# Unread TensorE products with 128 columns of weights in place of 32, in four places of a two-layer decoder kernel

## The reference

```python
logits = jnp.einsum('bsd,de->bse', x, Wg)          # routing, layer 0
top_vals, top_idx = jax.lax.top_k(logits, TOP_K)
...
att = jax.nn.softmax(jnp.einsum('blhd,bmhd->blmh', q, k) * scale, axis=2)   # cross attention
```

## Time and profile before

| what | us |
|---|---|
| median of three runs | 1131.32 |
| the three runs | 1131.32, 1134.64, 1130.4 |
| span of the profiled execution, first to last instruction (the profile gives no other time of it) | 1131.2 |
| TensorE busy in it (8612 products) | 1010.0 |
| weight loads, beside it | 719.1 |
| VectorE, ScalarE, GpSimd busy | 618.1, 425.0, 255.4 |
| mean granted clock of TensorE | 0.967 |

### The profile page before, as it was taken

One profiled execution on the slowest core, in us unless ns is written; L12 is line 12 of the kernel. 1 busy time (PEld: TensorE's weight loads), 2 busy tenths in 40 slices (PEclk: granted clock), 3 DMA queues, 4 the chain that ended last, 5 costly groups with the idle time before them and its releaser, 6 DMA issues.

```text
span 1131.2 us, 20802 instructions
## 1 busy us (share of the span) xinstructions
PE 1010.0 (89%) x8612; PEld 719.1 (64%) x8612; DVE 618.1 (55%) x1398; ACT 425.0 (38%) x557; POOL 255.4 (23%) x282
## 2 busy tenths in 40 slices
PE   6889889999987899999998798879888987986997
PEld 3666566576575799997445465747565665654566
DVE  2653753662667564333334846675575668765443
ACT  1533533524433355555541254142416231541112
POOL 0310310120130233333322020231013110210662
PEclk9999999899897899999999899999999999997999
DMA  6013413211400691111113000200020010004447
GB/s 188 1 43 126 135 43 107 89 43 44 152 1 1 254 378 57 47 48 47 43 39 98 1 2 6 85 2 5 1 76 2 6 38 1 1 2 131 130 135 236
DMA packets 64237, 80.50 MB, mean 71 GB/s; under 512 B 12736, under 2 KB 57680, under 8 KB 63120
## 3 DMA queue, kind: packets, MB, share of 16 engines
q1 hardware_dynamic: 53392, 61.15, 16.3%
q0 software_dynamic: 5664, 15.47, 4.2%
q10 hardware_dynamic: 5088, 2.56, 0.9%
HBM read 46.13 MB, written 33.03 MB: 70 GB/s over the span
## 4 chain that ended last, share of the span: by engine, by line
PE 61%; DVE 17%; ACT 12%; issue 5%; DMA 2%; POOL 2%; SPq 0%; ACTq 0%; DVEq 0%; POOLq 0%
PE ps L1522 8%; PE ps L1857 7%; DVE sb_arena L874 6%; ACT sb_arena L645 6%; PE ps L1658 5%; PE ps L1680 4%; PE ps L1885 4%; PE ps L1868 3%; PE ps L1728 3%; PE ps L1783 3%; DVE sb_arena L878 3%; PE ps L1566 2%; PE ps L1995 2%; PE ps L1630 2%; PE ps L1905 2%
## 5 line engine op out<-in xcount | busy, mean ns | idle before, releaser
L645 ACT ACTIVATE sb_arena<-ps 77x2048 f32<-77x2048 f32 (+1 forms) x64 | 116.5, 1880 | 27.9 <-PE ps L1612 26.7
L1388 POOL TENSOR_TENSOR sb_arena<-sb_arena,sb_neghalf 128x2 f32<-128x2 f32 x40 | 28.7, 719 | 397.2 <-DVE sb_arena L840 397.2
L1522 PE MATMUL ps<-sb_arena,sb_wreg 128*128 128x256 f32 (+1 forms) x512 | 110.8, 365 | 6.8 <-issue 3.8
L1522 PEld LDWEIGHTS ps<-sb_arena,sb_wreg 128*128 128x128 f32 (+1 forms) x512 | 89.0, 195 | 23.7 <-issue 8.3
L1857 PE MATMUL ps<-sb_arena 128*128 128x128 f32 x800 | 100.2, 280 | 3.2 <-ACT sb_arena L757 2.3
L1630 PE MATMUL ps<-sb_arena 32*77 32x256 f32 (+1 forms) x1024 | 78.4, 424 | 25.8 <-ACT sb_arena L645 13.1
L1857 PEld LDWEIGHTS ps<-sb_arena 128*128 128x128 f32 x800 | 97.0, 196 | 5.2 <-ACT sb_arena L757 2.9
L757 ACT ACTIVATE sb_arena<-sb_arena 128x1024 f32 x72 | 76.0, 1057 | 16.8 <-issue 12.4
L1630 PEld LDWEIGHTS ps<-sb_arena 32*77 32x77 f32 (+1 forms) x1024 | 44.3, 177 | 46.1 <-ACT sb_arena L645 24.2
L874 DVE TENSOR_REDUCE sb_arena<-ps 128x8 f32<-128x2048 f32 x32 | 71.0, 2282 | 3.5 <-PE ps L1586 3.5
L1566 PE MATMUL ps<-sb_headrow,sb_identb 128*32 128x512 bf16 (+1 forms) x266 | 65.8, 385 | 1.4 <-DVE sb_arena L878 1.3
(11 more groups left out here) (285 smaller groups left out, 1886.9 us busy)
## 6 DMA issues: line engine op xcount, KB each, us to landing
sb_arena<-in_m_w SPq DMA_DIRECT2D x8, 1536.0 KB, 9.8
sent<-sb_xres SPq DMA_DIRECT2D x32, 256.0 KB, 2.6
sb_arena<-outs SPq DMA_DIRECT2D x16, 512.0 KB, 6.0
outs<-sb_zeros SPq DMA_DIRECT2D x4, 1664.0 KB, 9.7
sent<-sb_zeros SPq DMA_DIRECT2D x2, 2560.0 KB, 13.7
sb_arena<-in_m_w SPq DMA_DIRECT2D x16, 256.0 KB, 3.4
early<-sb_xres SPq DMA_DIRECT2D x12, 256.0 KB, 2.9
sb_arena<-in_xT SPq DMA_DIRECT2D x8, 256.0 KB, 3.2
```

Of the source, the lines that this page charges most:

```text
L645: nc.scalar.activation(dst, src, ACT.Exp).then_inc(S(f"h_PT{p}"), 1)
L1522: ins = mm(dst[:, m * cols:(m + 1) * cols], wt[0:rows, k, m * P:(m + 1) * P], src[0:rows, k, 0:cols], start=(k == 0), stop=(k == KC - 1))
```

## The change

In four of its callers idle gets low=0: the whole identity as weights, and all 128 partitions of the bank written. Counts, moving operand, banks, places in the queue and waits stay as they are.

```diff
--- before.py
+++ after.py
@@ -1560,10 +1560,10 @@
                                      start=(k == 0), stop=(k == KC - 1))
                 ins.then_inc(S(f"h_kv{p}"), 1)
 
-            def idle(p, count, n=0, first=0):
+            def idle(p, count, n=0, first=0, low=IDLE):
 
                 for _ in range(count):
-                    ins = mm(bank(p, n)[IDLE:P, first:], identb[:, IDLE:P], headrow[:, :, :].rearrange("p g k -> p (g k)")[:, first:],
+                    ins = mm(bank(p, n)[low:P, first:], identb[:, low:P], headrow[:, :, :].rearrange("p g k -> p (g k)")[:, first:],
                              start=True, stop=True, skip_group_check=True)
                 return ins
 
@@ -1597,7 +1597,7 @@
             def shift_rows(p, n, c):
                 if not c.selfattn and p == 0:
                     pe.wait_ge(S(f"h_max{p}"), c.scores_at(n) + c.score_units)
-                    idle(p, IDLE_SPLIT)
+                    idle(p, IDLE_SPLIT, low=0)
                 pe.wait_ge(S(f"h_nmb{p}"), c.at(n) + 1)
                 nmb = bufs[p].nmbx if c.clip else bufs[p].nmb
                 for t in range(NT):
@@ -1683,7 +1683,7 @@
 
             def turn_result(p, n, c):
                 if n + 1 == PAIRS and p == 0:
-                    idle(p, IDLE_RESULT, 2)
+                    idle(p, IDLE_RESULT, 2, low=0)
                 pe.wait_ge(S(f"h_out{p}"), c.at(n) + 1)
                 if c is X0 and n + 1 < PAIRS:
                     pe.wait_ge(S(f"gla_act{p}"), GLA_ACT.done("g1", n + 1))
@@ -1695,7 +1695,7 @@
             def route(p, n, router):
                 pe.wait_ge(S(f"xoT{p}"), n + 1)
                 if n + 1 < PAIRS:
-                    idle(p, IDLE_ROUTE, 2)
+                    idle(p, IDLE_ROUTE, 2, low=0)
                 for t in range(NT):
                     for k in range(KC):
                         ins = mm(bank(p, 2)[:, t * E:(t + 1) * E], bufs[p].xoT[:, k, t * P:(t + 1) * P], router[:, k, :],
@@ -1765,7 +1765,7 @@
                 if n + 1 == PAIRS and p == 0:
                     pe.wait_ge(S("counts"), 1)
                 if p == 1:
-                    idle(p, IDLE_TURN, 2)
+                    idle(p, IDLE_TURN, 2, low=0)
                 for t in range(NT):
                     if t == 0:
                         pe.wait_ge(S(f"gla_pool{p}"), GLA_POOL.done("yn", n))
```

## The result

Eight runs of the changed kernel took 1122.33 to 1125.97 us, median 1123.81; eight of the kernel before 1125.38 to 1134.64, median 1131.2. The ratio is 0.9945, with a 95% interval of 0.993 to 0.9959: 0.55% faster, 6.2 us (the two medians alone differ by 7.4 us). "No change", which the forecast of 1131.3 stood for, is excluded by the interval. The gain has the size that rival A was given (1124.9), for another reason, so it is luck that the range, drawn down to A's price, takes in 1125.1.

The account below looks back on a forecast made before the run. The prediction took TensorE's time in order, and behind it its clock, to bound the kernel. Its terms, 0 + 0 + 0 + 0 on the profiled 1131.2 us, gave a forecast of 1131.3, range 1124.9 to 1136.0 us.

Parts of the forecast that it names:

- rival A: TensorE's clock: weight width counts at least a little, so two falls go, 6.4 us, to 1124.9; chance 0.10.
- The load: Weight loads of the 84 touched products: 99 ns at either width and hidden, change 0; upper bound 7.6 us.
- rival B: The 84 wide loads take the f32 row's time, unhidden: 7.6 us slower, 1138.9; chance 0.06.
- The product: The 84 touched products: paced by their 512 moving columns alone, 216 ns at either width; change 0.
- The neighbours: Touched products between products of 128 columns: no sharing of the array to lose; change 0.
- The clock: TensorE's granted clock: width doesn't count in what keeps it at 2.4 GHz; change 0.
- X: Not in the prediction; later guess: beside full-width products, a load of another width isn't overlapped; 1.4 us at routing.
- Rival C: Clock falls at other moments, two more or less in the typical run: 1124.5 or 1138.1; chance 0.06.

Follow-up runs that it names:

- e1: Separate kernel computing nothing of the reference: unread products of 32, 64 or 128 columns between other products, then bursts; a unit took 4.48, 4.51 and 4.08 us.
- e5: Separate kernel computing nothing of the reference: mixed units and timed bursts with unread products of 32 or 128 columns; a unit took 1.86 against 1.67 us.
- e9: The changed kernel itself, run again beside the kernel before: 1132.67 us, ratio 0.9953.
- e2: Kernel before with only the 12 unread products in front of routing widened to 128 columns: 1125.12 us, ratio 0.9961.
- e4: Kernel before with all 84 unread products given 64 columns of weights: 1130.46 us, ratio 0.9995 to the kernel before.
- e6: Changed kernel with 4 full-width unread products in front of each routing in place of 2: 1128.49 us, ratio 0.9982 to the kernel before.
- e8: Kernel before, all widths 32, with 3 unread products in front of each routing in place of 2: 1129.93 us, ratio 0.9996.
- e3: Kernel before with 72 of the 84 unread products widened to 128 columns, all but those in front of routing: 1129.71 us, ratio 0.9993.
- e7: Changed kernel with 1 full-width unread product in front of each routing in place of 2: 1122.96 us, ratio 0.993 to the kernel before.

## Why the prediction was right in time and wrong in kind

**The load: right.** 102 ns for 98; rival B, 67 ns shown per load, is out. The rule that spoke against the change, columns / 1.2 ns in the Trainium skill, "TensorE: Matmul & The Clock Gate", section "LDWEIGHTS (loading the stationary operand)", has no sign in these rows.

**The product: right.** The full-width groups keep their 216 ns: eleven recorded ones at the last turn_result take 2.54 us.

**The neighbours: the step that failed.** It said: "their own pace of 216 ns shows no sharing. Nothing is lost." I priced a narrow product by its pace among its like, and a wide load by its pace among its like, and took the sum for their meeting. I also had the neighbours wrong: the products ahead of the groups in shift_rows (L1591) and of each round's first group at routing (L1721) have 32 and 16 rows of weights, so there only the way out of the group becomes cheaper. The price lies at the meeting: 0.19 to 0.21 us there and back at the full clock beside full-width products, 0.40 at the lower. The trace of before had it in the open: two products of 0.22 us held 0.54 us of the chain and the router's eight 0.99 us at 0.11 us apiece, against 0.45 and 0.79 after. Counted from the profiles: 0.48 us in each of three rounds at routing (9.01 us for 9.49, above), about 0.09 us in each of eight shift_rows, about 0.19 us in each of two turn_result: 2.5 us.

**The clock: right that width doesn't count, probably wrong that the change to it is nothing.** e1's and e5's bursts show the first. But the changed kernel spends 6.0 +- 2.4 us less at the lower clock in the mean (e9), e2 7.1 +- 3.1; by the fitted slope these are 1.6 and 1.9 us. (For e9 X had said within 5 us, a cause in the clock about 9: its 6.0 decides neither.) Of the 29 us that go between the two profiles, 10 go at the routing of rounds 2 and 3, where the crossings stood; the others go elsewhere, some, as at 645 and 959 us, with no touched product ahead, so two profiles can't tell cause from chance. That the removed stalls cause the shorter low time is the plain reading, and e4, which keeps the stalls at another width and has 58.3 us for 59.7, agrees; it isn't shown, for e6 and e8 add products to the same stretch and gain little.

**The sum.** Of the 5.3 us that the runs of e9 measure (0.9953), 3.75 +- 0.55 are there at equal low time and 1.6 are the clock's; 2.5 are counted from the rows. Between 2.5 and 3.75 lies 1.2 us that stays open, and by e2 and e3 it lies at routing: e2 has 2.74 +- 0.33 for 1.4 counted, e3 0.40 +- 0.32 for 1.1. A part may be that a low stretch under L1728 costs more than the fitted 0.27 us per us: in round 2 it takes 10.03 - 8.68 = 1.35 us less, with 3.4 us at the lower clock where it had 204.3 - 198.25 = 6.05, about 0.5 us per us. Rival C, moments, is real as noise (the kernel before ran from 1125.16 to 1135.4 us in one batch) but is not the cause: the ratio came out the same in the runs of e9, 7 to 9 us slower for both kernels.

**The better version.** e7, one full-width product in front of each routing, has 0.993 to the changed kernel's 0.9945 and 0.9953. It beats the kernel before clearly; the intervals overlap, so whether it also beats the changed one isn't shown.

## What to carry to other kernels

Filler that keeps TensorE's clock up should be full-width between full-width products; between row-tiled ones of 32 rows its width made no difference in e1. Filler with the tiling of row-tiled neighbours was not run. Look for "issue" gaps of some 0.4 us on the weight-load side at a change of form; they point at a mixed sequence, which no mean by form shows. The gap is not itself the price: the product before it still runs in most of it, and the crossing there and back cost 0.19 to 0.21 us. Price an instruction in its place, from the start of its predecessor to the start of its successor, not by its pace in a row of its own kind.

## What the hardware showed that I had not expected

- A change of tiling, in rows or columns, keeps the next weight load from starting under the running product: 0.19 to 0.21 us there and back at 2.4 GHz, 0.40 us at 1.2 GHz, 64 columns like 32.
- In 17 of the 20 full-width groups of unread products the record of the first product is missing, behind row-tiled and full-width products alike, so counts of products are not to be trusted there; those of loads are (8612 in both).
- 84 products without a reader, some 18 us of TensorE's time, keep the clock up for about 75 us (133.4 us at the lower level without them, 57.8 with them) and make the kernel 1.7% faster than without (0.9953 / 1.0125).
